# Hybrid network kernel: experts of one image and projections of the next placed between the attention products of the present one

## Chip, cores, metric

One core of a Trainium2 chip. The metric is the device time of one execution in microseconds (us). Before the change the median of three runs is 10049.57 us (10046.44 to 10052.68).

## What is computed

The input is 16 images of 128 channels and 32 x 32 points. A first layer normalises them in groups and takes each of the 2048 matrices of 32 x 32 through a matrix logarithm, a subtraction of the mean and a matrix exponential; the change leaves this part as it is. A second layer takes each image as 1024 tokens of 128 channels:

```python
t = _to_tokens(x)
t = t + _L1_attn_ref(_ln_t(t), Wq, Wk, Wv, Wo, bo)   # 8 heads of 16, the 32 largest scores of each row, softmax
t = t + _L1_ffn_ref(_ln_t(t), gate_w, thr_w, fc1_w, lora_A, lora_B, fc2_w)   # 4 experts, gates with thresholds
x = _from_tokens(t, x)
```

The images are independent of each other here. The attention weighs the 32 largest scores of a row; the kernel weighs all 1024 with their exponentials where it can show that the rest is negligible (it keeps a measure of that in `w_widest`), and has a second, exact pass (`general`) behind a flag, which is not taken with these inputs.

## The kernel before, in words

`hybrid_kernel` first runs the matrix functions and then `attention_and_experts` (line 1760), which gives each engine one loop over the 16 images: `once` (line 1769) calls `pe_image`, `act_image`, `dve_image` and `sp_image` for image `b`. Each engine takes its instructions in this written order; only semaphores tie the engines to each other. `hold` (line 51) is a wait on a semaphore that the engine takes in order. PSUM has eight banks of 128 x 512 floats.

An image goes through these stages:

- Norm (`norm_pe`, `norm_act`, `norm_dve`): averages over channels by a matmul with a constant matrix (line 1267), centring on VectorE (1291), squares on ACT (1282), variances by 8 small matmuls (1271), the root by Ln and Exp on ACT (1284, 1286) and a refining step on VectorE (lines 63 to 69, 1298), a wide copy of it (1300), 8 matmuls that turn it (1276), and the product (1304).
- Projections (`project_pe`, line 1341, and its ACT and DVE halves): q and k, and v (1345), then q and k cut into three bf16 parts each (lines 1377, 1393, 1380, 1397). 32 chunks of three matmuls (`stack_pe`, line 1322) stack these parts to a depth of 96 for each head, 16 of them before the scores and 16 (`stack_late_pe`) beside the first scores; ACT and VectorE copy them out.
- Attention in four units (two groups of four heads by two halves of the queries). `fast_pe` makes five passes of 16 steps. In pass u a step makes scores for unit u (`score_pe`, two bf16 matmuls, line 1415, into the bank pairs 0, 1 and 2, 3 in turn) and two turned score tiles for unit u - 1 (line 1441, rotating through banks 4, 5, 6), whose exponentials ACT takes (1499), and two float products of these with the values into bank 7 (`weigh_pe`, line 1470). VectorE takes the eight largest of each 128 scores (MAX8, line 1520), eight MAX8 per step. The first pass has no products, and the fifth has no scores.
- Between passes: VectorE reduces the maxima of the unit and splits them into three bf16 rows (lines 1524 to 1531; the work up to 1541 is the measure of the rest), TensorE turns them (line 1458), ACT copies them under the queries (`shift_act`, line 1510), so that the turned scores come out with the maximum subtracted. The unit's sum is copied (1479), its denominators spread (`finish_pe`, line 1475), inverted by Ln and Exp on ACT (1481, 1483) and multiplied in on VectorE (1488).
- Join (line 1620) with the residual (1630), the second norm, gates (1637), the experts' hidden layer (1646), the low-rank layer (1653), the gates turned (1658), output (1663), the last sum (1725), and the store of the image (1755). At the end of the image TensorE waits until the last sum is done.

An image begins on an engine when the engine has finished the one before; nothing of two images runs at the same time.

Of the kernel before, what the change touches and what calls it, by code (L numbers as in the profile page):

```python
# [1251 lines left out]
def image_pass(nc, mem, w, s, out_dram, general):  # L1252

    banks = mem.banks
    first = B if general else 0


    def tokens(b):
        return mem.even[:, bass.ds(b - first, 1), :].rearrange("p m n -> p (m n)")

    def norm_pe(pe, n, source):

        for k in range(2):
            last = nc.tensor.matmul(banks[k][:], w.average[:], source[:, QB * k:QB * k + QB], start=True, stop=True)  # L1267
        last.then_inc(s.averaged, 1)
        hold(pe, s.squared, n + 1)
        for t in range(KT):  # L1270
            last = nc.tensor.matmul(banks[2][:, t:t + 1], w.squares[:, P * t:P * t + P], w.mean_column[:],  # L1271
                                    start=True, stop=True)
        last.then_inc(s.variances, 1)
        hold(pe, s.spread_ready, n + 1)
        for t in range(KT):
            last = nc.tensor.matmul(banks[t // 4][:, P * (t % 4):P * (t % 4) + P],  # L1276
                                    w.root_wide[:, t, :], mem.ident[:], start=True, stop=True)
        last.then_inc(s.scale_spread, 1)

    def norm_act(act, n):  # L1280
        act.wait_ge(s.centred, n + 1)
        nc.scalar.activation(w.squares[:], w.centred[:], ACT.Square).then_inc(s.squared, 1)
        act.wait_ge(s.stats, n + 1)
# [4 lines left out]
    def norm_dve(dve, n, source, result):  # L1288
        dve.wait_ge(s.averaged, n + 1)
        for k in range(2):  # L1290
            last = nc.vector.tensor_tensor(w.centred[:, QB * k:QB * k + QB], source[:, QB * k:QB * k + QB], banks[k][:],
                                           ALU.subtract)
        last.then_inc(s.centred, 1)
        dve.wait_ge(s.variances, n + 1)
        nc.vector.tensor_scalar(w.var[:], banks[2][:, 0:KT], EPS_LN, None, ALU.add).then_inc(s.stats, 1)
# [5 lines left out]
            .then_inc(s.spread_ready, 1)  # L1301
        dve.wait_ge(s.scale_spread, n + 1)
        for k in range(2):
            last = nc.vector.tensor_tensor(result[:, QB * k:QB * k + QB], w.centred[:, QB * k:QB * k + QB], banks[k][:],
                                           ALU.mult)
        last.then_inc(s.normal, 1)

    CHUNKS = 2 * HEADS * 2  # L1310
    EARLY = CHUNKS // GROUPS
    STACK_BANKS = (6, 7, 4, 5)
# [4 lines left out]

    def stack_pe(c):
        which, h, k = chunk(c)
        stack = (w.stack_q, w.stack_k)[which]  # L1320
        for part in range(3):
            last = nc.tensor.matmul(banks[STACK_BANKS[c % 4]][0:DEPTH, :], stack[:, h, part, :],  # L1322
                                    w.parts[:, which, part, QB * k:QB * k + QB], start=(part == 0), stop=(part == 2))
        last.then_inc(s.stacked, 1)

    def stack_late_pe(pe, b, n):
        if n >= 4:
            hold(pe, s.stack_out_late, b * (CHUNKS - EARLY) + n - 3)
        stack_pe(EARLY + n)

    def stack_late_act(act, b):
        for n in range(CHUNKS - EARLY):
            act.wait_ge(s.stacked, b * CHUNKS + EARLY + n + 1)
            nc.scalar.activation(stack_to(EARLY + n), banks[STACK_BANKS[n % 4]][0:DEPTH, :], ACT.Copy)\
                .then_inc(s.stack_out_late, 1)

    def project_pe(pe, b):
        hold(pe, s.normal, b * 2 + 1)
        for weight, first_bank in ((w.wq, 0), (w.wk, 2)):
            for k in range(2):  # L1340
                last = nc.tensor.matmul(banks[first_bank + k][:], weight[:], w.z[:, QB * k:QB * k + QB],  # L1341
                                        start=True, stop=True)
            last.then_inc(s.projected, 1)
        for t in range(KT):
            last = nc.tensor.matmul(banks[4 + t // 4][:, P * (t % 4):P * (t % 4) + P], w.z[:, P * t:P * t + P], w.wv[:],
                                    start=True, stop=True)
        last.then_inc(s.projected, 1)
        for c in range(EARLY):
            if c == 0:
                hold(pe, s.third_parts, b * 4 + 2)  # L1350
            if c == 8:
                hold(pe, s.third_parts, b * 4 + 4)
            if c == 2:
                hold(pe, s.v_out, b + 1)
            if c >= 4:
                hold(pe, (s.stack_out_act, s.stack_out_dve)[c % 2], b * 8 + (c - 4) // 2 + 1)
            stack_pe(c)
# [3 lines left out]
    def rests(c):  # L1361
        return w.att[:, c // 2, QB * (c % 2):QB * (c % 2) + QB]

    def part_of(c, part):
        return w.parts[:, c // 2, part, QB * (c % 2):QB * (c % 2) + QB]

    def stack_to(c):
        which, h, k = chunk(c)
        return (w.q, w.k)[which][0:DEPTH, h, QB * k:QB * k + QB]

    def factor_of(c):
        return float(DH) ** -0.5 if c < 2 else 1.0

    def project_act(act, b):
        for c in range(4):
# [30 lines left out]
    def where(u):  # L1406
        return u // 2, u % 2
# [467 lines left out]
```

## Time and profile before

| | |
|---|---|
| median of the runs | 10049.57 us |
| the profiled execution | 10055.52 us |
| its span | 10053.7 us |
| images part (from 4765.9 us) | 5287.8 us |
| mean granted TensorE clock | 0.923 |
| TensorE busy | 8488.0 us, 84% |
| VectorE busy | 5449.9 us, 54% |
| ACT busy | 4030.6 us, 40% |

Busy time of an engine is the time in which it executes matmuls or operations. The granted clock is a share of 2.4 GHz, and 0.5 is 1.2 GHz. A float matmul stands in the trace as two records (passes). L1470 is line 1470 of the kernel; a number of us from the span's start says when something happened.

### The profile page before, as it was taken

The page shows a single profiled execution, that of the slowest core. Times are in us where ns is not written, and L with a number is a line of the kernel's source. Part 1 is how long each engine was busy: PE and PEld are TensorE (multiplying, and loading weights), DVE is VectorE, ACT ScalarE, POOL GpSimd, SP SyncE. Part 2 cuts the span into 40 slices and gives each one's busy share as a digit, 9 for nine tenths or more (in the row PEclk, how much of TensorE's full clock was granted, in tenths as well). Part 3 has the DMA queues.
Part 4 walks back from the last instruction along what each step waited for, and adds up shares of the span by engine and source line. Part 5 has one row for each costly group of instructions (what it writes and reads, how often), then busy time and mean ns, then how long its engine had stood idle before and what let it go on. Part 6 is the DMA issues. An engine that isn't in the chain of part 4 may idle for free.

```text
span 10053.7 us, 604531 instructions
## 1 busy us (share of the span) xinstructions
PE 8488.0 (84%) x266476; PEld 4549.5 (45%) x266476; DVE 5449.9 (54%) x15245; ACT 4030.6 (40%) x7646; POOL 1958.2 (19%) x2042
## 2 busy tenths in 40 slices
PE   3999999999997794885888888889888888888888
PEld 2677777777776674774222222222222222222222
DVE  4677777777764565332544355435543554445444
ACT  3455555555543341443433343334333333333333
POOL 1555555555553351000000000000000000000000
PEclk9999999999998896997988998899889998999989
DMA  0000000000000000001000000000000000000000
GB/s 34 1 0 0 0 0 0 0 0 0 0 0 0 0 1 2 0 0 38 1 3 3 3 1 3 3 3 1 3 3 3 1 3 3 3 1 3 3 3 3
DMA packets 9779, 32.20 MB, mean 3 GB/s; under 512 B 1525, under 2 KB 3130, under 8 KB 9274
## 3 DMA queue, kind: packets, MB, share of 16 engines
q1 hardware_dynamic: 9274, 26.02, 0.7%
q8 instruction: 249, 4.08, 0.2%
q14 instruction: 256, 2.10, 0.1%
HBM read 17.63 MB, written 8.39 MB: 3 GB/s over the span
## 4 chain that ended last, share of the span: by engine, by line
PE 41%; DVE 6%; ACT 3%; issue 2%; DVEq 0%; ACTq 0%
PE psum L1470 20%; PE psum L1441 6%; PE psum L1415 4%; DVE w_best L1520 4%; PE psum L1322 2%; PE psum L1646 1%; ACT w_q L1510 1%; PE psum L1276 1%; PE psum L1653 1%; PE psum L1267 1%; PE psum L1271 1%; PE psum L1341 1%; PE psum L1620 1%; PE psum L1475 1%; PE psum L1637 0%
## 5 line engine op out<-in xcount | busy, mean ns | idle before, releaser
L1520 DVE MAX8 w_best<-psum 128x8 f32<-128x128 f32 x8192 | 1695.3, 280 | 1011.3 <-PE psum L1415 1010.9
L1470 PE MATMUL psum<-w_exp,w_v 128*32 128x512 f32 x4096 | 2123.7, 620 | 6.9 <-ACT w_exp L1499 4.4
L1499 ACT ACTIVATE w_exp<-psum 128x512 f32<-128x512 f32 x2048 | 1210.8, 597 | 1749.9 <-PE psum L1441 1749.9
L1441 PE MATMUL psum<-w_q,w_k 99*128 99x512 bf16 x2048 | 805.6, 400 | 42.9 <-ACT w_q L1510 42.9
L1415 PE MATMUL psum<-w_k,w_q 96*128 96x512 bf16 x2048 | 629.9, 390 | 205.2 <-ACT w_q L1510 116.0
L499 PE MATMUL psum<-e_prod_u,e_j 32*32 32x64 f32 x49152 | 769.7, 215 | 30.5 <-ACT e_prod_u L579 25.1
L499 PEld LDWEIGHTS psum<-e_prod_u,e_j 32*32 32x32 f32 x49152 | 707.8, 105 | 182.1 <-issue 182.1
L1441 PEld LDWEIGHTS psum<-w_q,w_k 99*128 99x128 bf16 x2048 | 200.3, 98 | 1194.6 <-issue 1101.7
L653 POOL TENSOR_TENSOR e_diag<-odd,e_eye 128x512 f32<-128x512 f32 x384 | 488.8, 1273 | 560.2 <-PE psum L473 522.1
L547 ACT ACTIVATE e_square<-e_off 128x512 bf16<-128x512 f32 x384 | 242.1, 630 | 845.0 <-POOL e_off L657 845.0
L1470 PEld LDWEIGHTS psum<-w_exp,w_v 128*32 128x32 f32 x4096 | 277.1, 109 | 655.8 <-issue 655.8
L382 PE MATMUL psum<-e_mix,e_zs 32*32 32x32 f32 x49152 | 509.4, 196 | 60.4 <-issue 58.8
L1415 PEld LDWEIGHTS psum<-w_k,w_q 96*128 96x128 bf16 x2048 | 127.3, 97 | 914.4 <-issue 903.4
L382 PEld LDWEIGHTS psum<-e_mix,e_zs 32*32 32x32 f32 x49152 | 477.2, 107 | 107.4 <-issue 107.1
L606 DVE TENSOR_TENSOR e_j<-e_rest,psum 128x512 f32<-128x512 f32 x384 | 264.2, 688 | 468.2 <-PE psum L382 468.2
L382 PE MATMUL psum<-e_x 32*32 32x32 f32 x49152 | 504.6, 195 | 14.2 <-issue 13.8
L382 PE MATMUL psum<-e_j,e_a_fixed 32*32 32x32 f32 x49152 | 495.9, 194 | 18.7 <-issue 14.2
L951 PE MATMUL psum<-power 32*32 32x32 f32 x28672 | 392.1, 206 | 120.3 <-issue 113.3
L382 PEld LDWEIGHTS psum<-e_j,e_a_fixed 32*32 32x32 f32 x49152 | 462.5, 104 | 62.1 <-issue 30.0
L663 POOL TENSOR_TENSOR e_x_eye<-e_x,e_eye 128x512 f32<-128x512 f32 x384 | 488.7, 1273 | 2.3 <-DVE e_x L634 2.3
L657 POOL TENSOR_TENSOR e_off<-odd,e_not_eye 128x512 f32<-128x512 f32 x384 | 488.3, 1272 | 0.0
L382 PEld LDWEIGHTS psum<-e_x 32*32 32x32 f32 x49152 | 472.0, 106 | 31.0 <-issue 15.8
(282 smaller groups left out, 11945.0 us busy)
## 6 DMA issues: line engine op xcount, KB each, us to landing
odd<-in_x SPq DMA_DIRECT2D x1, 8192.0 KB, 23.1
even<-in_x SPq DMA_DIRECT2D x1, 8192.0 KB, 23.3
out<-w_t SPq DMA_DIRECT2D x16, 512.0 KB, 4.8
w_hid<-in_fc SPq DMA_DIRECT2D x2, 256.0 KB
w_wo<-in_wo SPq DMA_DIRECT2D x8, 8.0 KB
w_wq<-in_wq SPq DMA_DIRECT2D x1, 64.0 KB
w_wk<-in_wk SPq DMA_DIRECT2D x1, 64.0 KB
w_wv<-in_wv SPq DMA_DIRECT2D x1, 64.0 KB
```

Source lines behind the costliest of these rows:

```text
L382: last = nc.tensor.matmul(bank[rows, cols], left[rows, cols], right[rows, cols], start=True, stop=True)
L499: last = nc.tensor.matmul(halves(e.pair[:, k // HALF, :])[rows, :, to], e.j[rows, cols], e.prod_u[rows, :, cols], start=True, stop=True)
L606: nc.vector.tensor_tensor(e.j[:], e.rest[:], banks[TURN], ALU.add).then_inc(turned, 1)
L653: nc.gpsimd.tensor_tensor(as_matrices(e.diag[:]), as_matrices(e.a_at(t)), over_matrices(e.eye[:]), ALU.mult)\
L657: nc.gpsimd.tensor_tensor(as_matrices(e.off[:]), as_matrices(e.a_at(t)), over_matrices(e.not_eye[:]), ALU.mult)\
L663: nc.gpsimd.tensor_tensor(as_matrices(e.x_eye[:]), as_matrices(e.x[:]), over_matrices(e.eye[:]), ALU.add)\
L951: last = nc.tensor.matmul(banks[EXP_BANK[n]][rows, S * k:S * k + S], left[rows, k, :], right[rows, k, :], start=True, stop=True)
L1415: last = nc.tensor.matmul(banks[2 * (i % 2) + k][:], w.q[0:DEPTH, 4 * g + j, q0:q0 + P], w.k[0:DEPTH, 4 * g + j, QB * k:QB * k + QB], star ...
L1441: nc.tensor.matmul(banks[4 + m % 3][:], w.k[0:DEPTH + SHIFT_ROWS, 4 * g + j, P * kt:P * kt + P], w.q[0:DEPTH + SHIFT_ROWS, 4 * g + j, QB * ...
L1470: nc.tensor.matmul(banks[7][slot(j), :], w.v[:, kt, 4 * g + j, :], w.exp[m % 4][:], start=(kt == 0), stop=(kt == KT - 1)).then_inc(s.weigh ...
L1499: nc.scalar.activation(w.exp[m % 4][:], banks[4 + m % 3][:], ACT.Exp).then_inc(s.exp_done, 1)
L1520: last = nc.vector.max(w.best[:, i, o, :], banks[2 * (i % 2) + o // 4][:, P * (o % 4):P * (o % 4) + P])
```

## The change

One function, `image_pass`, is written anew. All stages are cut into small helpers (`average_pe`, `variances_pe`, `spread_pe`, `join_pe`, `gates_pe`, `hidden_pe`, `low_pe`, and their ACT and DVE halves), with the same operations. There are now four passes ("phases") per image, of 16 steps. Phase p of image b makes the scores of unit p of image b and the products of the unit before it; in phase 0 this is the last unit of image b - 1. The step's order on TensorE is: scores, a turned score tile, a product of an earlier tile, side work, a turned tile, a product. The side work of phase 1 is the second half of the values and the 16 late stacks of image b, and the join, norm, gates and half of the hidden layer of image b - 1; of phase 2 the rest of the experts of b - 1 and the beginning of the norm of image b + 1; of phase 3 the rest of that norm, projections and the 16 early stacks of b + 1.

The banks are dealt anew. Scores have banks 0 and 1 alone, so score i + 1 waits for the MAX8 of score i (before: score i - 1). Turned tiles rotate through banks 4 and 5. Norms, projections, early stacks, join and experts use 2 and 3 (`PAIR`), bank 6 (`EXTRA`) takes late stacks and other small results. The values are made in two groups, 8 matmuls of 64 columns each (before: 8 of 128). The k projection waits for the rests of q. A unit's denominators and inverse are made in the first step of the pass after the products' own. Products 30 and 31 follow after step 15, and the turning of the maxima stands between these two. The first and the last image are written out without a loop, and 14 images are in a loop. Norm, projections and early stacks of image 0 stand before it all; the last unit's products and the last image's join and experts follow behind it, one after the other.

```diff
-    def fast_pe(pe, b):
-        base = b * UNITS
-        for u in range(UNITS + 1):
-            for i in range(16):
-                if u < UNITS:
-                    n = 16 * u + i
-                    if i >= 2:
-                        hold(pe, s.read_max, b * 64 + n - 1)
-                    elif i == 0 and u >= 1:
-                        hold(pe, s.shifted, base + u)
-                    score_pe(pe, b, u, i)
-                if u == 0:
-                    stack_late_pe(pe, b, i)
...
+    def beside_pe(pe, b, phase, i, back, front):
+        behind, ahead = b - 1, b + 1
+        n_back, n_front = b * 2, b * 2 + 1
+        if phase == 1:
+            if i == 0:
+                values_pe(PAIR[0], 1)
+            stack_late_pe(pe, b, i)
+            if back:
+                if i == 2:
+                    hold(pe, s.v_out, b * 2 + 2)
+                    join_pe(pe, behind, 0)
+                elif i == 3:
+                    join_pe(pe, behind, 1)
+                elif i == 5:
+                    hold(pe, s.residual, behind * 2 + 2)
+                    average_pe(n_back, w.t)
+                elif i == 7:
+                    variances_pe(pe, n_back)
+                elif i == 10:
+                    spread_pe(pe, n_back)
+                elif i == 12:
+                    gates_pe(pe, behind, n_back)
+                if i >= 12:
+                    hidden_pe(pe, behind, i - 12)
+        if phase == 2 and back:
+            if i < 4:
+                hidden_pe(pe, behind, i + 4)
+            elif i < 8:
+                for e in (2 * (i % 2), 2 * (i % 2) + 1):
+                    low_pe(pe, behind, (i - 4) // 2, e)
+            elif i == 8:
+                gates_turned_pe(pe, behind)
+            elif i == 9:
+                expert_out_pe(pe, behind)
+        if phase == 2 and front:
+            if i == 11:
...
+                average_pe(n_front, tokens(ahead))
+            elif i == 13:
+                variances_pe(pe, n_front)
+        if phase == 3 and front:
+            if i == 0:
+                spread_pe(pe, n_front)
+            elif i == 2:
+                project_pe(pe, ahead, 0, n_front)
+            elif i == 4:
+                project_pe(pe, ahead, 1, n_front)
+            elif i == 5:
+                values_pe(EXTRA, 0)
+            elif i >= 8:
+                for c in (2 * (i - 8), 2 * (i - 8) + 1):
+                    stack_early_pe(pe, ahead, c)
...
+    def phase_pe(pe, b, phase, back, front, scored=True):
+        at = b * UNITS + phase
+        before = at - 1
+        weighs = back or phase >= 1
+        closes = back or phase >= 2
+        unit = (phase - 1) % UNITS
...
+        for i in range(16):
+            if i == 0 and scored:
+                beside_pe(pe, b, phase, i, back, front)
+            if i == 0 and weighs:
+                hold(pe, s.shifted, at)
+            if scored:
+                if i >= 1:
+                    hold(pe, s.read_max, at * 16 + i)
+                score_pe(phase, i, 0)
+            for x in (2 * i, 2 * i + 1):
+                if weighs:
+                    scores_t_pe(pe, before, unit, x)
+                if x == 0 and closes:
+                    denominators_pe(pe, before - 1)
+                if weighs and x >= 2:
+                    weigh_pe(pe, before, unit, x - 2, not closes)
+                if x % 2 == 0 and i >= 1 and scored:
+                    beside_pe(pe, b, phase, i, back, front)
+        if weighs:
+            weigh_pe(pe, before, unit, 30, not closes)
+        if scored:
+            if weighs:
+                hold(pe, s.exp_done, before * 32 + 32)
+            turn_maxima_pe(pe, at)
+        if weighs:
+            weigh_pe(pe, before, unit, 31, not closes)
...
+    def images(eng, phase):
+        for u in range(UNITS):
+            phase(eng, 0, u, False, True)
+        with eng.Fori(1, B - 1) as b:
+            for u in range(UNITS):
+                phase(eng, b, u, True, True)
+        for u in range(UNITS):
+            phase(eng, B - 1, u, True, False)
+        phase(eng, B, 0, True, False, scored=False)
...
+    def fast_pe(pe):
+        front_pe(pe, 0, 0)
+        images(pe, phase_pe)
+        denominators_pe(pe, LAST)
+        hold(pe, s.den_inverse, LAST + 1)
+        back_pe(pe, B - 1, 2 * B - 1)
```

ACT's side work (`beside_act`) stands behind both exponentials of a step: in phase 1 the copy of a late stack in each step, the squares at step 6, the root at 8, the gates' exponentials at 12, hidden tiles at 12 and 14; in phase 2 hidden tiles at 0 and 2, low tiles at 5 and 7, squares at 12, the root at 14; in phase 3 the first parts at 2 and 4, the second parts at 3 and 6, the values at 5, copies of stacks from 8 on. VectorE's (`beside_dve`) stands behind the step's eight MAX8: in phase 1 the residual at 2 and 3, centring at 5, variance at 7, the root at 8, the norm's product at 10, logits at 12, hidden tiles at 13 and 15; in phase 2 hidden tiles at 1 and 3, the gates' softmax at 4 and weights at 6, the mix at 8, the last sum at 9, centring at 11, variance at 13, the root at 14; in phase 3 the norm's product at 0, first rests at 2 and 4, third parts at 5 and 7, copies of stacks from 8 on. The operations between passes keep their order on VectorE. On ACT, the shift rows come first and the copy of the sum after them. SP issues one store per image, as before.

## Rows read from the trace of the kernel before

**Rows 1.** The page's busy time: us, share of the span and instructions of each engine

```profile
PE 8488.0 (84%) x266476; PEld 4549.5 (45%) x266476; DVE 5449.9 (54%) x15245; ACT 4030.6 (40%) x7646; POOL 1958.2 (19%) x2042
```

**Rows 2.** Line 1755, the stores: ns min/median/max, first and last start

```profile
L1755 SPq DMA_DIRECT2D out<-w_t x16: 332/332/354, 5092.4 to 10047.3; - x16
```

**Rows 3.** Stages of one image: stretch, its length, busy of each engine, clock, DMA

```profile
5096.70:5134.00 37.30, 28.11 (x109) 17.59 (x110) 14.81 (x27) 11.43 (x21) 0.00 (x0) 0.77 0.00 1
5134.00:5166.40 32.40, 21.54 (x96) 9.51 (x96) 29.96 (x141) 11.53 (x20) 0.00 (x0) 0.93 0.00 1
...
5221.50:5275.70 54.20, 50.82 (x146) 10.52 (x146) 32.03 (x142) 22.75 (x39) 0.00 (x0) 0.97 0.00 1
...
5330.00:5372.80 42.80, 41.83 (x96) 7.38 (x96) 0.00 (x0) 18.89 (x32) 0.00 (x0) 0.96 0.00 1
5372.80:5376.80 4.00, 1.10 (x2) 0.32 (x3) 0.69 (x1) 1.82 (x3) 0.00 (x0) 0.98 0.00 0
5376.80:5423.50 46.70, 35.23 (x112) 17.58 (x112) 13.70 (x36) 5.37 (x11) 0.00 (x0) 0.83 0.00 1
5423.50:5429.70 6.20, 0.00 (x0) 0.00 (x0) 0.00 (x1) 0.00 (x0) 0.00 (x0) 0.50 0.26 91
```

**Rows 4.** The chain in order of time, between two images: start, us, what

```profile
5092.28 4.45 issue
```

**Rows 5.** The same chain, one step in the middle of unit 2

```profile
5248.28 0.54 PE psum L1415 x2
5248.81 0.22 PE psum L1441
...
5250.01 0.32 PE psum L1441
...
5251.31 0.54 PE psum L1415 x2
```

**Rows 6.** The timeline of one step: start, us, engine, line, operation

```profile
5206.20 0.61 PE L1415 MATMUL psum<-w_k,w_q 96*128 96x512 bf16 x2
...
5206.95 1.68 DVE L1520 MAX8 w_best<-psum 128x8 f32<-128x128 f32 x8 [1.35 <-PE psum L1415]
5207.06 0.60 ACT L1499 ACTIVATE w_exp<-psum 128x512 f32<-128x512 f32 x1 [1.14 <-PE psum L1441]
```

**Rows 7.** The timeline between two units, from the last MAX8 on

```profile
5214.73 0.38 DVE L1524 TENSOR_REDUCE w_top<-w_best 128x16 f32<-128x128 f32 x1
...
5216.56 0.19 DVE L1531 TENSOR_TENSOR w_shift<-w_minus,w_shift 128x16 bf16<-128x16 f32 x1
...
5217.98 1.05 PE L1458 MATMUL psum<-w_ident,w_shift 128*3 128x128 bf16 x16
...
5219.37 2.04 ACT L1510 ACTIVATE w_q<-psum 3x512 bf16<-3x512 f32 x4
5220.40 0.17 DVE L1541 SCALAR_TENSOR_TENSOR w_widest<-w_eighth,w_widest 128x16 f32<-128x16 f32 x1
```

**Rows 8.** Timeline, the experts' part: float passes; and the chain, the 16 early stacks

```profile
5388.42 1.92 PE L1271 MATMUL psum<-w_mean_column,w_squares 128*128 128x1 f32 x16 [2.56 <-ACT w_squares L1282]
5398.32 1.92 PE L1637 MATMUL psum<-w_gates_t,w_z 128*128 128x5 f32 x16 [1.47 <-DVE w_z L1304]
5409.35 7.08 PE L1653 MATMUL psum<-w_hid,w_lora_a 128*64 128x512 f32 x16
...
5122.58 10.55 PE psum L1322 x48
```

**Rows 9.** Timeline, VectorE's first and last operation for the root

```profile
5391.06 0.20 DVE L63 RECIPROCAL w_var_spare<-w_root 128x8 f32<-128x8 f32 x1 [0.52 <-ACT w_root L1286]
...
5392.27 0.69 DVE L1300 COPY w_root_wide<-w_root 128x1024 f32<-128x1024 f32 x1
```

**Rows 10.** Stretch behind a gap between two units, columns as in rows 3

```profile
5223.00:5226.00 3.00, 2.98 (x6) 0.46 (x5) 2.55 (x13) 1.22 (x3) 0.00 (x0) 0.51 0.01 3
```

**Rows 11.** The chain in the pass of scores alone, one step

```profile
5137.32 1.47 DVE w_best L1520 x8
```

More of the change, by code:

```diff
@@ L1312, in image_pass, with rests, part_of, factor_of @@
-    STACK_BANKS = (6, 7, 4, 5)
+    def rests(c):
+        return w.hid[:, c, :]
+    def part_of(c, part):
+        return w.parts[:, c // 2, part, half(c % 2)]
+    def factor_of(c):
+        return float(DH) ** -0.5 if c < 2 else 1.0
+    def project_pe(pe, b, which, n):
+        if which == 0:
+            hold(pe, s.normal, n + 1)
+        else:
+            hold(pe, s.first_rests, b * 4 + 2)
+        for k in range(2):
+            last = nc.tensor.matmul(banks[PAIR[k]], (w.wq, w.wk)[which][:], w.z[:, half(k)], start=True, stop=True)
+        last.then_inc(s.projected, 1)
@@ L1321, in stack_pe, with stack_to @@
         for part in range(3):
-            last = nc.tensor.matmul(banks[STACK_BANKS[c % 4]][0:DEPTH, :], stack[:, h, part, :],
-                                    w.parts[:, which, part, QB * k:QB * k + QB], start=(part == 0), stop=(part == 2))
+            last = nc.tensor.matmul(banks[stack_bank(c)][0:DEPTH, :], stack[:, h, part, :],
+                                    w.parts[:, which, part, half(k)], start=(part == 0), stop=(part == 2))
         last.then_inc(s.stacked, 1)
+    def stack_to(c):
+        which, h, k = chunk(c)
+        return (w.q, w.k)[which][0:DEPTH, h, half(k)]
@@ L1326, in stack_late_pe @@
     def stack_late_pe(pe, b, n):
-        if n >= 4:
-            hold(pe, s.stack_out_late, b * (CHUNKS - EARLY) + n - 3)
+        if n >= 1:
+            hold(pe, s.stack_out_late, b * (CHUNKS - EARLY) + n)
         stack_pe(EARLY + n)
[L1331 to L1357, printed above, removed]
+    def stack_late_act(act, b, n):
+        act.wait_ge(s.stacked, b * CHUNKS + (EARLY + n + 1))
+        nc.scalar.activation(stack_to(EARLY + n), banks[EXTRA][0:DEPTH, :], ACT.Copy).then_inc(s.stack_out_late, 1)
@@ L1358, in project_pe, with stacks_ready @@
+    def stacks_ready(pe, b):
         for out in (s.stack_out_act, s.stack_out_dve):
             hold(pe, out, b * 8 + 8)
[L1361 to L1372, printed above, removed]
@@ L1473, in finish_pe @@
[L1473 to L1482 removed]
+        hold(pe, s.exp_done, at * 32 + (x + 1))
@@ new lines, in shift_act, with denominators_pe @@
+    def shift_act(act, at, u):
+        g, qb = where(u)
+        act.wait_ge(s.max_turned, at + 1)
+        for j in range(4):
+            last = nc.scalar.activation(w.q[DEPTH:DEPTH + SHIFT_ROWS, 4 * g + j, half(qb)],
+                                        banks[SHIFT_BANKS[j]][DEPTH:DEPTH + SHIFT_ROWS, :], ACT.Copy)
+        last.then_inc(s.shifted, 1)
+    def denominators_pe(pe, at):
+        hold(pe, s.gathered, at + 1)
+        nc.tensor.matmul(banks[7], w.select[:], w.o[:], start=True, stop=True).then_inc(s.den_spread, 1)
```

771 lines of the change are left out of this document (478 added, 293 removed).

## Prediction

> **What bounds the kernel now.** I read the page first: TensorE is busy 84% of the span [rows 1]. Then the output transfers, one per image: 16 of them, the first issued at 5092.4, the last at 10047.3 [rows 2]. So an image takes (10047.3 - 5092.4) / 15 = 330.3 us, and the sixteen images together 5288 of the 10053.7 us. The change touches these alone. The stage windows of one image [rows 3] show where its 330 us lie. 37.3 us go to the front (norm, projections, early stacks), with TensorE busy 28.1 of them at a granted clock of 0.77. Then 32.4 us hold scores without value products, bound by VectorE. Three units of scores beside products take 54 us each (one shown), with TensorE busy 50.8. The fourth unit's products alone take 42.8, closing it 4.0, joining and experts 46.7 (TensorE 35.2, clock 0.83). Between the last sum of an image and the next image's first matmul there is nothing at all, for 4.45 us here [rows 4] and 6.2 us one image later [rows 3].
>
> The step of a middle unit is a pure TensorE chain, and one comes every 5251.31 - 5248.28 = 3.03 us [rows 5], and VectorE's eight MAX8 take only 1.68 of it [rows 6]. So the bound is TensorE inside the units, and a chain through all three engines outside them. The change attacks the second kind of time.
>
> **The change, part by part, for an image in the loop.**
>
> 1. Five passes over the units become four: the next image's first scores run beside the last products. The pass of 32.4 us without products goes. What stays is 4 x 16 steps of 3.03 = 194 us. The step's length rests on one thing the trace doesn't show: scores now have one pair of banks, so score i+1 waits for the maxima of score i. Here are the times within a step: VectorE starts 0.75 after the scores' start and needs 1.68 [rows 6]; with 0.15 for the signal that is 2.6 us, before the 3.03 at which TensorE comes back. Bounds for the extra wait are 0 (there is a margin of 0.4 us; a gain is excluded, since the same products fill the step) and 0.5 us per step, if VectorE starts late in each. I take 0, since side work on TensorE lengthens the same step. The two-bank rotation for the transposed scores costs nothing either: the first exponential of a step starts 0.86 us into it and takes 0.60 [rows 6], and its bank is wanted again in the next step.
>
> 2. Closing work per pass. Turning the maxima is 1.05 us [rows 7], the denominators 0.88 (two passes of 0.44, below): 4 x 1.93 = 7.7 us, now all on TensorE's line.
>
> 3. Side work, costed as TensorE time, since it now stands between products in the same queue. A 512-column float pass costs 7.08 / 16 = 0.44, a weight-bound small one 1.92 / 16 = 0.12, three stack passes 10.55 / 16 = 0.66 [rows 8]. Stacks 32 x 0.66 = 21.1; join 8 passes, both averages 8, the two projections 8, hidden 16, expert output 4: 44 x 0.44 = 19.4; low 7.0; variances, scale spreading (twice each), gates and gate turning, 6 x 1.9 = 11.4 (the spreading row stands at half clock now); value projections, now in two groups of 64 columns with twice the weight loads, 2 x 1.9 = 3.8. Sum 62.7 us. Next to it each piece changes between bf16 and float, which costs 0.1 us (a pass of 0.22 takes 0.32 when the float product follows at once [rows 5]). The last products of a pass, which follow each other with no scores between, give about as much back; I count both as nothing.
>
> 4. Work moved to ACT and VectorE. VectorE is free in a step from 2.44 to 3.78 us (0.75 + 1.68, then the next scores plus 0.75), 1.3 us, more when the step has TensorE side work. Most pieces (1.3 us for two tensor operations, 0.7 for a copy) fit and cost nothing; without that cover each would cost its own length. Three don't fit. The root: ACT can start it only after its two exponentials, and VectorE's part runs from the end of ACT's Exp to the end of the wide copy, 1.9 us [rows 9]. In pass 1 that makes the next maxima late and TensorE waits about 0.8 for them. In pass 2 it stands at step 14 of 16 and goes on into the closing chain. The first rests in pass 3 wait for ACT's first parts: twice 0.65.
>
> 5. Waits at a pass's end. From the end of the last maxima (5214.7) to the finished split at 5216.75 VectorE needs 2.06 us [rows 7]; TensorE has one product pair of cover left, so it waits about 0.8, and 2.1 in pass 2. Then the shift rows: ACT needs 2.04 plus signals after the turning [rows 7]; one product (0.9) and the first side piece cover it in passes 1 and 3, leaving 0.5 before pass 2. The first step then waits 0.8 to 1.05 for its own maxima, as little stands between scores 0 and 1. VectorE's remaining maxima work reaches 3.8 us past the split [rows 7] and just clears. Sum of points 4 and 5: root and rests 0.8 + 1.3, starts 4 x 1.05, ends 3 x 0.83 + 2.1, shift 0.5 = 11.4 us.
>
> 6. The loop's return stays, once per image. All engines take it with their queues empty. It is not a wait for a neighbour: the chain calls it issue [rows 4]. The rows give 4.45 and 6.2 us and bound it; I take 4.5, which an undisturbed chain shows, plus 1.7 for the clock (between units a stretch at half clock follows the gap, 3 us of it shown [rows 10], some 3.4 in all, and half of it is lost), plus 1.8 because VectorE and ACT return later than TensorE: 8.0. It stands on TensorE's line between the scores; nothing covers it. The Trainium skill, Advanced Engine Details and Errata, Control Flow Timing, gives a compare-and-branch about 108 ns; by that price alone this term would be 4 us less per image, but the measured 4.45 us decides.
>
> Sum: 194 + 7.7 + 62.7 + 11.4 + 8.0 = 283.8 us against 330.3. By passes, each 48.5 + 1.9 and then its side work and waits: phase 0 has 0 + 1.9 + 8.0, together 60.3; phase 1 27.0 + 2.7, 80.1; phase 2 17.9 + 3.7, 72.0; phase 3 17.9 + 3.2, 71.5. The stored image's DMA stays once per image and has most of a pass before its buffer is wanted.
>
> The ends. The first front is 42 us instead of 37.3: the key projection now waits for the query's rests, and two stack banks instead of four add waits of 0.1 to 0.3 per chunk. The first image has a pass with scores alone: 0.75 + 1.47 [rows 11] + 0.15 = 2.4 us per step, so 16 steps are 38, with the closing 43, and 7 more if the clock falls to half; 50. Phase 1 without the join and what follows is 48.5 + 1.05 + 12.5 (values, stacks) + 2 = 64; phase 2 has only the next norm beside it, 48.5 + 1.9 + 3.7 + 3.7 = 58; phase 3 is whole, 71.5. So 243. Fourteen loop images: 14 x 283.8 = 3973. The last image has no return before it and no successor: 52.3 + 80.1 + 67 (72.0 less the norm's 3.7 and its root's 1.3) + 53.7 (no side work, but the shift's wait uncovered) = 253. Then products alone, closing, experts as now, 42.8 + 4.0 + 46.7 [rows 3], and 6.6 us of tail: 100. Together 42 + 243 + 3973 + 253 + 100 = 4611 against 5288, so 677 us less: span 9377, time of that execution 9379 (10055.5 for a span of 10053.7 before). The median of the runs shown is 6 us below the profiled execution, so 9373.
>
> **Rivals.**
>
> A. The clock falls at every pass's end, not only at the loop's return. For it: between two units now, where TensorE does little more than the turning in 5 us [rows 7], the clock falls to 0.51 [rows 10]. Against it: the new gaps are 0.8 to 2 us with work between. Price 3 x 1.7 x 15 = 77 us: 9450, more if it also falls within passes. The Trainium skill, TensorE: Matmul & The Clock Gate, section "A second HAM failure mode: psum-queue depth-cycling", says that short idles between matmul groups, one group per bank rotation, can make the clock go back and forth; in the middle units here, which rotate three banks, the trace shows 0.97 over a whole stage [rows 3]. Chance 0.14.
>
> B. Side pieces hold TensorE. Each exchange (about 20 per image) exposes a microsecond because ACT answers only behind its exponentials: 20 x 14 = 280 us, 9653. For it: ACT and VectorE take their side work in a fixed order, each behind the step's own. Against it: most pairs are placed one to three steps apart. Chance 0.12.
>
> C. Slower. The single pair of score banks serialises the step: TensorE waits for the maxima in each step rather than working on products meanwhile. Fully serial it is 0.75 + 1.68 + 2.6 = 5.0 us, 64 x 5.0 + 62.7 + 7.7 + 19.4 = 410 per image, 11270 us in all. It decides from (330.3 - 62.7 - 7.7 - 8.0) / 64 = 3.94 us per step, that is 0.9 us of wait in each. The products stand in the queue between two scores, which speaks against it. Chance 0.03.
>
> D. Waits of point 5 vanish and the return's clock loss too: 10 to 14 us less per image, about 9200. Chance 0.08.
>
> The forecast, 9280 to 9470, keeps 0.63. A range of 9280 to 9600 takes in A and the nearer half of B. No other case ends near zero change; a measurement here tells 0.2% (20 us) from nothing, and I leave 0.01 for it.
>
> **What the changed profile should show.** Output transfers 284 us apart; a middle step without side work still 3.03 us; TensorE busy over 90% of a loop image with a clock above 0.95; no stage without products between the first and the last image; one gap of 4 to 6 us per image with nothing to wait for; waits of scores on MAX8 only at a pass's first steps and behind the roots. I am wrong if the plain step is over 3.2 us, if the clock is 0.5 after each pass, or if waits on ACT or VectorE in a loop image sum to over 25 us.

## The result, and the profile after

The changed kernel takes 9332.97 us (median of four runs, 9329.91 to 9336.33), against 10048.01 of the kernel before on the same chip: a ratio of 0.9288 (95% interval 0.9272 to 0.9304). The forecast was 9373 in a range of 9280 to 9600. The profiled execution's span is 9334.6 us; the images part starts at 4770.9, so it takes 4563.7 us where the sum said 4611 and the kernel before took 5287.8.

The page's busy time and slices, after:

```profile
PE 8227.5 (88%) x266349; PEld 4441.4 (48%) x266732; DVE 5465.7 (59%) x15245; ACT 3963.6 (42%) x7646; POOL 1955.6 (21%) x2042
...
PE   3899999999998779478759999999999999999998
...
PEclk9999999999999889689869999999999999999999
```

VectorE and ACT have nearly the busy time of [rows 1] in a shorter span. TensorE's own busy time even fell by 260 us; the granted clock rose from 0.923 to 0.954 on average, so less of the work was done at 1.2 GHz, which would account for a fall, but how much of the 260 it makes was not shown. The last 19 slices of TensorE have no digit below 8.

The turnings of the maxima are the milestones of this kernel, one per phase. Here they are in the timeline of one loop image (start in us, duration, and in brackets how long the engine was idle before it and whom it waited for):

```profile
5337.84 1.05 PE L1491 MATMUL psum<-w_ident,w_shift 128*3 128x128 bf16 x16 [1.95 <-DVE w_shift L1533]
...
5395.60 1.05 PE L1491 MATMUL psum<-w_ident,w_shift 128*3 128x128 bf16 x16 [1.54 <-DVE w_shift L1533]
...
5474.18 1.05 PE L1491 MATMUL psum<-w_ident,w_shift 128*3 128x128 bf16 x16 [1.61 <-DVE w_shift L1533]
...
5546.07 1.87 PE L1491 MATMUL psum<-w_ident,w_shift 128*3 128x128 bf16 x16 [2.81 <-DVE w_shift L1533]
...
5618.61 1.05 PE L1491 MATMUL psum<-w_ident,w_shift 128*3 128x128 bf16 x16 [1.95 <-DVE w_shift L1533]
```

Their differences are the lengths of the phases: 57.8, 78.6, 71.9 and 72.5 us, in all 280.8. The prediction by phases was 60.3, 80.1, 72.0 and 71.5, 283.8 in all. The last four of the bracketed waits, those of this image, sum to 7.9 us. The other loop images have phases 1 and 2 of the same length (one phase 2 took 73.5), while phase 0 varies between 55.9 and 57.9 us and phase 3 between 71.0 and 73.8. The first image of the loop has no return before it, and its phase 0 takes 53.0. In this image, up to 5618.6, TensorE is busy 94% at a clock of 0.99.

A plain step of phase 0, in the timeline (compare [rows 5, 6]):

```profile
5641.18 0.61 PE L1465 MATMUL psum<-w_k,w_q 96*128 96x512 bf16 x2
...
5641.94 1.68 DVE L1932 MAX8 w_best<-psum 128x8 f32<-128x128 f32 x8 [1.34 <-PE psum L1465]
5642.04 0.60 ACT L1915 ACTIVATE w_exp<-psum 128x512 f32<-128x512 f32 x1 [1.13 <-PE psum L1474]
```

In the chain, two such steps begin 5650.34 - 5647.31 = 3.03 us apart, as before:

```profile
5647.31 0.54 PE psum L1465 x2
...
5650.34 0.54 PE psum L1465 x2
```

Who waited for whom in 277 us, from early in phase 1 to phase 1 of the next image (total us, times, longest); these are the rows of TensorE's matmuls, and just before the stretch stands one more wait, of 0.2 us, for ACT's copy of a late stack:

```profile
PE psum L1491 <- DVE w_shift L1533: 7.9, 4, 2.8
...
PE psum L1465 <- DVE w_best L1932: 5.2, 7, 1.7
...
PE psum L1465 <- issue: 2.7, 1, 2.7
...
PE psum L1465 <- ACT w_q L1499: 0.3, 1, 0.3
```

7.9 + 5.2 + 0.3 = 13.4 us of waits for a neighbour against 11.4 predicted. The 1.7 us of the longest wait for MAX8 stand behind the loop's return, so the prediction has them in its term for the return. The row of 2.7 is the return itself. Its timeline:

```profile
5621.76 0.60 ACT L1511 ACTIVATE w_o<-psum 128x512 f32<-128x512 f32 x1
5622.12 0.17 DVE L1543 SCALAR_TENSOR_TENSOR w_widest<-w_eighth,w_widest 128x16 f32<-128x16 f32 x1
5623.18 0.59 PE L1465 MATMUL psum<-w_k,w_q 96*128 96x512 bf16 x2 [2.66 <-issue]
...
5624.10 0.60 ACT L1915 ACTIVATE w_exp<-psum 128x512 f32<-128x512 f32 x1 [1.75 <-PE psum L1474]
...
5625.53 1.68 DVE L1932 MAX8 w_best<-psum 128x8 f32<-128x128 f32 x8 [3.24 <-issue]
...
5627.36 1.01 PE L1465 MATMUL psum<-w_k,w_q 96*128 96x512 bf16 x2 [1.68 <-DVE w_best L1932]
...
5632.09 0.61 PE L1465 MATMUL psum<-w_k,w_q 96*128 96x512 bf16 x2
```

TensorE is idle for 2.66 us here, not 4.45 as in [rows 4]; VectorE comes back last, its first MAX8 stands 2.35 us behind the scores, and the second scores wait 1.68 us for it, at half clock (1.01 us for the pair; the granted clock from 5625 to 5631 is 0.50). The sign "one gap of 4 to 6 us per image" was therefore a miss: the gap is there, but shorter.

### The profile page after: what moved, and what is told of

It reads as the page before. It is cut to its first block and busy times, and to the rows that moved or that the text cites. A ratio compares the mean times of both kernels' runs of the same rounds, so it can differ in the third digit from the quotient of the medians.

```text
span 9334.6 us, 604193 instructions
## 1 busy us (share of the span) xinstructions
PE 8227.5 (88%) x266349; PEld 4441.4 (48%) x266732; DVE 5465.7 (59%) x15245; ACT 3963.6 (42%) x7646; POOL 1955.6 (21%) x2042
## 5 line engine op out<-in xcount | busy, mean ns | idle before, releaser
L1932 DVE MAX8 w_best<-psum 128x8 f32<-128x128 f32 x8192 | 1724.4, 283 | 1289.5 <-PE psum L1465 1244.0
L1484 PE MATMUL psum<-w_exp,w_v 128*32 128x512 f32 x4096 | 2096.1, 610 | 1.0 <-ACT w_inverse L1517 1.0
L1465 PE MATMUL psum<-w_k,w_q 96*128 96x512 bf16 x2048 | 628.0, 389 | 156.2 <-DVE w_best L1932 114.0
L382 PE MATMUL psum<-e_mix,e_zs 32*32 32x32 f32 x49152 | 509.8, 196 | 62.7 <-issue 61.3
```

Source lines behind the costliest of these rows:

```text
L382: last = nc.tensor.matmul(bank[rows, cols], left[rows, cols], right[rows, cols], start=True, stop=True)
L1465: last = nc.tensor.matmul(banks[base + k], w.q[0:DEPTH, 4 * g + j, q0:q0 + P], w.k[0:DEPTH, 4 * g + j, half(k)], start=True, stop=True)
L1484: nc.tensor.matmul(banks[7][slot(j), :], w.v[:, kt, 4 * g + j, :], w.exp[x % 4][:], start=(kt == 0), stop=(kt == KT - 1)).then_inc(s.weigh ...
L1932: last = nc.vector.max(w.best[:, i, o, :], banks[o // 4][:, P * (o % 4):P * (o % 4) + P])
```

## Experiments

Times are medians. The runs stand on several chips. The kernel before, run beside them, took 10049 us beside e1, e4, e6 and e7, and 10060 to 10066 beside the others. The changed kernel, run again on the chip of e9, took 9334.69 us, ratio 0.9277 (0.9262 to 0.9293), so a difference of a few us between chips is nothing:

> The changed kernel, unedited, on the chip of e9_blocks_phase1, to compare like with like: 0.929 of the kernel before, 9330 to 9350.

### The loop's return

```diff
-        with eng.Fori(1, B - 1) as b:
+        for b in range(1, B - 1):
             for u in range(UNITS):
                 phase(eng, b, u, True, True)
```

> The changed kernel with its 14 middle images written out without a loop. In the changed kernel's trace a phase 0 behind a loop return lasts 57.6 us from turning to turning, and one without a return before it 53.0. Theory 1: the return costs this difference and straight-line code costs nothing: 13 returns x 4.6 = 60 us less, 9333 becomes 9273. Theory 2, the term as predicted (8.0 us): 104 us less, 9229. Theory 3: fetching the code of an image costs the same written out: no change, 9333.

Measured: 9268.32 us, ratio 0.9227 (0.9212 to 0.9243), 65 us less than the changed kernel. Theory 1 holds. In every loop image phase 0 now takes 52.9 or 53.0 us; with a return it took 55.9 to 57.9. Over the 14 loop images the phases 0 sum to 740.7 us against 799.0, so the 13 returns cost 58.3 us, 4.5 each. The two traced spans differ by 66.8 us (9334.6 against 9267.8), and the rest of that isn't the return's: the traced run of e1 comes out of the matrix functions, which the edit doesn't touch, 8.1 us sooner (VectorE's copy L1178 begins at 4758.49 against 4766.54), and the rest of the images part differs by less than a microsecond in all.

```profile
5602.73 1.05 PE L1491 MATMUL psum<-w_ident,w_shift 128*3 128x128 bf16 x16 [1.60 <-DVE w_shift L1533]
...
5606.00 0.59 PE L1465 MATMUL psum<-w_k,w_q 96*128 96x512 bf16 x2 [1.36 <-ACT w_q L1499]
...
5608.57 0.59 PE L1465 MATMUL psum<-w_k,w_q 96*128 96x512 bf16 x2 [0.63 <-DVE w_best L1932]
...
5611.58 0.61 PE L1465 MATMUL psum<-w_k,w_q 96*128 96x512 bf16 x2
...
5655.60 1.05 PE L1491 MATMUL psum<-w_ident,w_shift 128*3 128x128 bf16 x16 [1.54 <-DVE w_shift L1533]
```

Set beside the return's timeline above, these rows split its cost. From the turning to the first scores it is 4.57 us with a return and 3.27 without, 1.3 more: the gap of 2.66 takes the place of a wait of 1.36 for the shift rows. From the first scores to the second it is 4.18 against 2.57, 1.6 more, mostly VectorE's late return. From the second to the third it is 4.73 against 3.01, 1.7 more, which is the half clock. Together 4.6. Where the clock doesn't fall behind the return, as in the next image, phase 0 takes 55.9 us and the return 3.0.

### The roots' place

```diff
@@ phase 2, TensorE (ACT: squares 12 -> 11, root 14 -> 12; VectorE: centring 11 -> 10, variance 13 -> 12, root 14 -> 13)
-            if i == 11:
+            if i == 10:
                 average_pe(n_front, tokens(ahead))
-            elif i == 13:
+            elif i == 12:
                 variances_pe(pe, n_front)
@@ phase 1, VectorE
-            elif i == 8:
+            elif i == 9:
                 root_dve(dve, n_back)
```

> The changed kernel with the two roots moved: in phase 1 VectorE's part a step later (9, not 8), in phase 2 the next image's average a step earlier (10), variances at 12, ACT's root at 12 and VectorE's at 13. Theory 1: the waits of 0.8 us (phase 1) and 1.3 (phase 2) vanish, and with the shorter gap behind phase 2 the stretch at half clock there (3.4 us, half of it lost): 3.8 us x 15 = 57 us less, 9276. Theory 2: the waits vanish and the clock falls as before: 30 us less, 9303. Theory 3: another wait takes their place: 9333.

Measured: 9293.36 us (9276.04 to 9294.97), ratio 0.9247 (0.9231 to 0.9262): 40 us less, between theories 1 and 2. In the trace, phase 1 falls from 78.6 to 78.2, phase 2 from 71.9 to 70.6 in most images (72.2 in some), and phase 3 from between 71.0 and 73.8 to 71.0 (17 us less over the 14 loop images). The turning behind phase 2 waits 1.54 us instead of 2.81 and runs at full clock, here and in all other images (compare the fourth turning above):

```profile
5536.19 1.05 PE L1491 MATMUL psum<-w_ident,w_shift 128*3 128x128 bf16 x16 [1.54 <-DVE w_shift L1533]
```

So the root's lateness behind phase 2 was 1.3 us as predicted, and in phase 1 the move took off only 0.4 where 0.8 was predicted.

### What side work and VectorE's time cost

```diff
-        stack_pe(EARLY + n)
+        stack_pe(EARLY + n, 2)       # for part in [0, 1, 2] * times
```

> The changed kernel with the three matmuls of each late stack made twice, into the same bank. Theory 1, side work costs its TensorE time in full: 16 x 0.66 = 10.5 us per image, 168 us more, 9501. Theory 2, TensorE has hidden slack in phase 1 because it waits for others there: 0 to 60 us more.

Measured: 9497.09 us, ratio 0.9455 (0.9439 to 0.9471), 164 us more. Phase 1 grows from 78.6 to 88.6 us, by 10.0, in every loop image, 140 us over the 14; the other three phases together change by 10. TensorE's time is paid in full.

```diff
+                for o in range(2):
+                    nc.vector.max(w.spare[:, i, o, :], banks[0][:, P * o:P * o + P])
                 for o in range(OCTANTS):
                     last = nc.vector.max(w.best[:, i, o, :], ...)
```

> The changed kernel with ten MAX8 per step instead of eight (two results go to a spare tile), 0.42 us more for VectorE in each step, 27 us per image. Theory 1, the plain step is bound by TensorE with a margin of 0.4 us: the steps cost nothing more, and only the places where VectorE is awaited do, some 12 per image (first and last step of a phase, roots, rests): 5 us per image, 80 us more, 9415. Theory 2, VectorE or the single pair of score banks bounds the steps: 27 x 16 = 430 us more, 9765. Theory 3, no place waits for VectorE: 9333.

Measured: 9427.21 us, ratio 0.9385 (0.9369 to 0.9401), 94 us more, about theory 1's 80 and far from 430. The steps of phase 0 are still 3.03 us apart; timeline of one of them, with the two extra ones in front:

```profile
5661.80 0.50 DVE L1933 MAX8 w_spare<-psum 128x8 f32<-128x128 f32 x2 [0.95 <-PE psum L1466]
...
5662.21 1.67 DVE L1935 MAX8 w_best<-psum 128x8 f32<-128x128 f32 x8
...
5664.07 0.60 PE L1466 MATMUL psum<-w_k,w_q 96*128 96x512 bf16 x2
```

VectorE ends at 5663.88 and the next scores start 0.19 us later, about the 0.14 that the signal takes, so the margin of 0.4 us is all but used up, and was real. The 94 us lie at the ends and in the places behind side work: each phase of a loop image grows by 1 to 2 us.

### One pair of score banks, in the kernel before

```diff
-                    if i >= 2:
-                        hold(pe, s.read_max, b * 64 + n - 1)
+                    if i >= 1:
+                        hold(pe, s.read_max, b * 64 + n)
@@ score_pe, then the MAX8 (lines shortened)
-            last = nc.tensor.matmul(banks[2 * (i % 2) + k][:], ...
+            last = nc.tensor.matmul(banks[(2 * (i % 2) if general else 0) + k][:], ...
-                    last = nc.vector.max(w.best[:, i, o, :], banks[2 * (i % 2) + o // 4][:, ...])
+                    last = nc.vector.max(w.best[:, i, o, :], banks[o // 4][:, ...])
```

> The kernel before, with scores in one pair of banks (0 and 1), so that a score waits for the maxima of the one before it. Theory 1, as predicted: the middle units' step stays at 3.03 us, as products stand between two scores, and only the pass of scores alone grows, from 1.58 to about 2.4 us per step (0.75 + 1.47 + 0.15): 13 us per image, 210 us more than before, 10258. Theory 2, the single pair serialises the middle units too: in each of 48 steps at least 0.5 us more, 24 us per image on top, 10640 or more.

Measured: 10446.24 us, ratio 1.0386 (1.0369 to 1.0403). That is 383 us more than before, where theory 1 said 210 and theory 2 at least 380 on top. By the time alone neither holds; the steps decide it: in the middle units they stay 3.03 us apart, so nothing serialises there, and the units grow only at their ends (56 to 58 us from turning to turning, 53 to 56 before, some 7 us for the three units). The rest of the 24 us per image, some 17, is in the pass of scores alone and around it. Its chain:

```profile
5890.19 1.02 PE psum L1415 x2
...
5891.35 1.70 DVE w_best L1520 x8
5893.04 0.14 issue
5893.18 1.03 PE psum L1415 x2
```

A step of it takes 5893.18 - 5890.19 = 2.99 us, not 2.4. Two things had been left out of the 2.4: TensorE, idle for two thirds of the step, falls to half clock (1.02 us for a pair that takes 0.6), and eight MAX8 that begin after a pause take 1.70, not the 1.47 of [rows 11], where they follow each other without one.

### The two halves of the change

First the interleaving undone. All engines do the join and experts of the image before as one block behind step 2 of a phase, and the next image's front as one block in phase 3 (TensorE's part of the edit; the side work it replaces is taken out, and ACT and VectorE have the like):

```diff
+    def block_pe(pe, b, phase, back, front):
+        behind, ahead = b - 1, b + 1
+        if phase == 2 and back:          # e9: phase == 1, and one more hold, on the late stacks
+            hold(pe, s.v_out, b * 2 + 2)
+            back_pe(pe, behind, b * 2)
+        if phase == 3 and front:
+            hold(pe, s.v_out, b * 2 + 2)
+            front_pe(pe, ahead, b * 2 + 1)
```

> The changed kernel with its four passes, but the previous image's join and experts as one unbroken block behind step 2 of phase 2, and the next image's norm, projections and early stacks as one behind step 2 of phase 3, on every engine. Theory 1, the gain of the change has two parts that add: per image 4 x 52.3 (steps, turning, denominators, waits of the start and end) + 4.6 + 12.5 (values and late stacks) + 46.7 + 37.3 (the blocks as in the kernel before) = 310 us, so 30 x 15 = 450 us more than the changed kernel, 9780. Theory 2, most of the gain is in the passes and the blocks run warm and short: at TensorE's own time it would be 280 + 10 = 290, 9480. Theory 3, almost all of the gain is in the interleaving: 320 or more per image, 9930.

Measured: 9889.14 us, ratio 0.9828 (0.9811 to 0.9845), between theories 1 and 3. This version takes half of one head group for its join from the wrong image, with the same amount of work; the next one reads the right one:

> As e2_blocks, but with the join and experts of the image before as one block behind step 2 of phase 1, ahead of the point where the present image's first unit is written over its attention output (in e2_blocks the block stood behind that point, so the join read one half of one head group from the wrong image; the amount of work was the same). Theory 1, what e2_blocks showed is the price of unbroken blocks (103 and 94 us for the passes with a block against 72 with the work spread, and 64 against 79 for phase 1): the same sum, 9880 to 9900. Theory 2, the place of the block matters: in phase 1 it lies before the late stacks and in a longer phase, over 40 us apart from e2_blocks either way.

Measured: 9903.6 us, ratio 0.9838 (0.9821 to 0.9854). The place matters little (14 us, on two chips). Against the changed kernel on the same chip it is 569 us more, 38 us for each image but the first, above the 30 of theory 1 of e2. The phases of one image are 57.9, 114.0, 52.9 and 95.8 us: phase 2, with no side work left, lasts exactly what phase 0 lasts without a return. The chain in the block of phase 1 shows what is paid:

```profile
5459.09 1.29 DVE w_centred L1303 x2
5460.41 1.06 ACT w_squares L1292
...
5461.61 3.56 PE psum L1279 x16
5465.19 0.18 DVE w_var L1308
5465.39 0.22 ACT w_root L1296
...
5467.18 0.70 DVE w_root_wide L1315
5467.88 0.14 issue
5468.02 3.62 PE psum L1286 x16
5471.66 1.30 DVE w_z L1321 x2
```

Each hand-over is one after the other, and the small matmuls, 1.68 and 1.78 us in the changed kernel, take 3.56 and 3.62 at a fallen clock (0.74 on average from 5455 to 5475).

Then the passes parted again, with the side work left in its steps (the last image, outside the loop, is parted in the same way):

```diff
         with eng.Fori(1, B - 1) as b:
-            for u in range(UNITS):
+            phase(eng, b, 0, True, True, scored=False)
+            phase(eng, b, 0, False, True)
+            for u in range(1, UNITS):
                 phase(eng, b, u, True, True)
```

> The changed kernel with the side work where it is, but the first scores of an image no longer beside the last products of the one before: products alone, then scores alone. Theory 1: instead of 57.6 us per image, products alone as in the kernel before (42.8) and scores alone with one pair of banks (16 x 2.4 + closing 4.5 = 43) and the return: 90 us, 32 us more per image x 15 = 480 us, 9815. With the clock at half in the scores (one matmul pair of 0.43 at 1.2 GHz more per step, 7 us): 9920. Theory 2: the first scores were cheap to hide and the loss is only the former pass of 32.4 us less what the step gained: 15 x 15 = 225 us more, 9560.

Measured: 9975.99 us, ratio 0.9912 (0.9892 to 0.9933): 643 us more than the changed kernel, 42.9 for each image but the first, more than the 32 of theory 1 and the 39 of its case at half clock. One image's two separate passes, cut in the middle (window, length, busy of PE, PEld, DVE, ACT, POOL, clock, DMA):

```profile
5696.68:5745.00 48.32, 45.19 (x118) 9.24 (x118) 4.09 (x10) 23.23 (x40) 0.00 (x0) 0.96 0.01 2
5745.00:5793.00 48.00, 14.77 (x30) 2.03 (x30) 28.02 (x135) 0.00 (x0) 0.00 (x0) 0.53 0.00 0
```

The second is the pass of scores alone: TensorE busy 31%, clock 0.53, 2.99 us per step as in e3. Phase 1 behind it takes 82.3 us instead of 78.6.

Each half alone thus leaves only 1 to 2% of a gain of 7%. Both undone:

> Both halves of the gain undone in the changed kernel: join and experts as one block in phase 1, the next image's front as one block in phase 3 (as e9_blocks_phase1), and products and first scores in passes of their own (as e5_separate_passes). Theory 1, the two halves add, and the changed kernel's new bank layout by itself costs 34 us per image against the kernel before (24 by e3_one_pair_before, and 10.5 for late stacks that stood beside scores alone and now stand between products): 9335 + 569 + 643 = 10547, over the kernel before by 480. Theory 2, the halves hide the same time and don't add, so that without both the kernel is back at the kernel before: 10050 to 10100.

Measured: 10529.92 us, ratio 1.0472 (1.0454 to 1.0489), against 10547 by the sum. Theory 1 holds: the halves add (569 + 643 us). They lie in different phases: phase 0 takes 97 us on average in e5 and in e12, and phases 2 and 3 take 52.9 and 94 in e12, 52.9 and 95 in e9. Underneath the halves some 470 us are left against the kernel before on the same chip, which this rewriting costs by itself. Two pieces of it have a price: one pair of score banks (383, e3) and late stacks that now stand between products (16 x 10.5 = 168 by the predicted price, 160 by e6). 383 + 168 = 551 is more than 470, so those two are not additive, or something else in the new order gives 80 us back; no run tells which.

### A faster version

Unrolled and with the roots moved:

> The changed kernel written out without a loop and with the two roots moved. If the two parts are independent: 60 + 57 us less than the changed kernel, 9216. If the clock stretch behind phase 2 doesn't go: 9243. If neither helps: 9333.

Measured: 9233.41 us, ratio 0.9182 (0.9167 to 0.9197).

> The kernel of e8_unrolled_roots again, beside the changed kernel on one chip: 0.918 of the kernel before, 100 us less than e10_changed_again. If the difference of e8_unrolled_roots to the changed kernel came from the chip, it is under 50 us here.

Measured: 9236.14 us, ratio 0.9177 (0.9162 to 0.9193), 98.6 us less than the changed kernel on the same chip. It beats both kernels, and lies between the first two cases of e8; the gains of e1 and e4, 65 and 40, nearly add. In the trace of e8 a loop image takes 272.4 us at best, where TensorE's own work by the prediction's prices is 194 + 7.7 + 62.7 = 264.4. Two of these phases, 3 and 0, with the clock at 1.00 (columns as above):

```profile
5525.70:5596.40 70.70, 67.26 (x235) 20.80 (x236) 43.50 (x161) 31.18 (x56) 0.00 (x0) 1.00 0.00 1
5596.40:5649.20 52.80, 49.30 (x146) 10.31 (x147) 31.90 (x142) 22.78 (x39) 0.00 (x0) 1.00 0.00 1
```

## Why the prediction was right, and where it wasn't

- **The step (point 1)** was right: 3.03 us, no extra wait. Shown by the traces of the changed kernel and of e3, and its margin by e7.
- **TensorE's line (points 2 and 3)** was right. The late stacks cost 10.0 us per repetition against 10.6 taken; values in 64 columns took 2.00 us (1.9 taken); the turning 1.05. By phases, summed over the 14 loop images, phase 1 came out 21 us shorter than predicted, phase 2 equal and phase 3 10 us longer, so these lines are right to within 2 us a phase, and not better. That each hand-over between bf16 and float is paid back by the closing products can be seen only in the sum; what pays it back is in the last section.
- **Waits (points 4 and 5)**: 13.4 us against 11.4, about right in sum, with errors each way that partly cancel, which is luck. The root in phase 1 and the rests in phase 3 were priced at 0.8 and twice 0.65; the timeline shows waits of 0.32 and 0.18 there. The first steps' waits for their own maxima are 0.68 three times, 0.97 once (phase 3, second step) and 1.68 behind the return, 4.7 in all against 4.2. The turnings together waited 7.9 us, where I had 4.6: VectorE's part was as reckoned (last MAX8 done at 5393.41, split done at 5395.46 in the first of them), but TensorE was done earlier, because products 29 and 30 stand side by side (last section), so they covered nearly a microsecond less.
- **The return (point 6)** was the mis-sized term: 8.0 us taken, 4.5 measured on average (e1), 4.6 in the image shown. Of its three parts the clock's (1.7 taken, 1.7 measured) and VectorE's late return (1.8 taken, 1.6 measured) were right; the idle time of TensorE was not. 4.5 was taken as it stood between two images of the kernel before, and 1.3 measured: the gap is 2.66 us here, and it takes the place of a wait of 1.36 for the shift rows, which are copied during it. In the sum, 14 returns at 8.0 are 112 us, while 13 came to 58, 54 less; that the whole sum was off by only 47 is because all the rest, with errors both ways, came out 7 longer. The 108 ns that the Trainium skill, Advanced Engine Details and Errata, Control Flow Timing, gives for a compare-and-branch would have erred on the other side: 13 returns at that price are 1.4 us, where 58 were measured.
- **The first image and the ends**: front 43 us (42 taken), scores alone 52.0 (50 taken). The latter came out by luck, as e3 shows: a step takes 2.99 us, 48 us for 16, where 38 and a separate 7 us for the clock were added. In the experiments on the separate pass (e3, e5) the same 2.4 made my forecasts too low.
- **Rival A**, the clock at each phase's end, was partly true. Behind phase 2, whose turning waited 2.81 us in every loop image, the turning ran wholly or partly at half clock in nine of the 14 (1.87 us in the image shown); behind phase 3, with a wait of 1.95, in three; behind phases 0 and 1, with waits of 1.5 and 1.6 us, in none. The same wait thus goes once with a fall and once without. The roots' move, which shortens the wait behind phase 2 (e4), left no slow turning behind a phase of a loop image and took 17 us off phase 3, which supports the link and sizes this part of the rival: 17 us, where 77 was its price. The clock of the phases' windows in the image shown is 0.97 to 1.00.
- **Rivals B, C and D** fell. B by the waits' sum; C by e7 and the 3.03 us; D, since the waits are there.

## What to carry to other kernels

Where one engine is to be the only bound, price every piece of moved work at that engine's time from a warm row, then walk the other engines' instructions step by step to see whether an answer is due before it can come; here such a sum hit within half a per cent, helped by errors that cancelled (54 us too much for the returns, some 7 too little elsewhere). A layout that merges stages costs something of its own (one pair of banks, copies that lose their cheap place), so half of such a change may show almost nothing: measured alone, each half left 1 to 2% of a gain that together is 7%. And look at what still breaks the chain, here a loop's return of 4.5 us and a root one step too late: together they gave another 1%. A gap read from the old kernel is not the price of the same gap in the new one: ask which wait it takes the place of.

## What the runs showed that I had not expected

- A loop's return left TensorE idle for 4.45 to 6.2 us in the kernel before, where all engines took it empty, but for 2.66 us in the image shown of the changed kernel. That it is shorter because the return begins while the last product is still being computed is my reading; no run shows it. VectorE was the last to be back (first MAX8 2.35 us after the scores). TensorE itself lost only 1.3 us by its gap; VectorE's delay and the half clock behind it made the rest of the 4.6.
- Two products issued next to each other run at the same time in the trace. Within a step the two products stand apart, and one takes 1.04 us in the timeline. At a phase's end products 29 and 30 follow each other directly; they go to different groups of 32 output partitions (heads 1 and 2 of their group) and take no longer together, four passes (two products) in 1.05 us, against two passes in 1.04:

```profile
5641.93 1.04 PE L1484 MATMUL psum<-w_exp,w_v 128*32 128x512 f32 x2
...
5393.01 1.05 PE L1484 MATMUL psum<-w_exp,w_v 128*32 128x512 f32 x4
```

  At every moment from 5393.01 to 5394.06 the trace has two of the four passes open. The ends of matmuls are modelled in it, but the starts aren't: in the kernel before, where products 29, 30 and 31 follow each other, the weights of the third are loaded 0.81 us after the first has begun (5215.12 against 5214.31), when the first two are all but done; one after the other they would take 1.9. The Trainium skill, TensorE: Matmul & The Clock Gate, Part 3, says that matmuls into distinct column groups run concurrently; the rows agree. An order in which all products of a step or two stand together, for four heads at once, may be worth far more than what is left in this one. It was not tried, so nothing here shows its gain.
- Writing 14 images out as straight code, all different instructions, cost nothing that can be seen: the phases without a return keep their length (78.6, 71.6 to 73.5, 70.7 to 72.5 us).
- Eight MAX8 take 1.47 us in an unbroken run [rows 11] and 1.67 to 1.70 in the rows shown where VectorE has waited for the scores, in the kernel before too [rows 6]. A step that makes VectorE wait pays 0.2 us for it.
- TensorE kept at about 30% busy, in pairs of matmuls every 3 us, was granted half clock for nearly a whole pass (0.53), and its pairs took 1.02 us instead of 0.6, which lengthens the step on which both engines wait.
